# GpSimd pauses after every fourth gather of a group in the edge passes of a graph network

## The chip, the cores and the metric

One core of a Trainium2 chip runs the whole program. Its engines are TensorE (PE), VectorE (DVE), ScalarE (ACT), GpSimd (POOL) and SyncE (SP), each with its own instruction stream; 16 DMA engines serve them all. The metric is the device time of one execution in microseconds.

## The reference, cut to what matters

The reference chains four graph layers over 6250 nodes of 128 features and 100000 edges, sorted by destination. The change lies in the code of the first two.

```
# first network: 4 layers of attention over the edges
scores = sum(Q[dst] * K[src], -1) * scale
e = exp(scores - segment_max(scores)[dst]);  attn = e / segment_sum(e)[dst]
messages = segment_sum(attn * V[src], dst)
h = layernorm(h + messages @ WO + bO)
# second network: 8 heads of 16 features, 2 relations
score = sum(q[dst] * k_r[src], -1) ...;  alpha = e / den[dst]
out += segment_sum(v_r[src] * alpha, dst)
```

For each edge, then, a row of a node table is fetched by the number of its source node, multiplied with a row of its destination, turned into a weight, and the weighted rows are added up by destination. The third and fourth networks are sums over edges as well, in another function.

## The kernel before, in words

The edges of the first two networks are laid out in a list of *groups*. A group has S = 16 columns of 128 edges, one edge to each of the 128 partitions. `edge_pass` (L1797) walks the list two groups at a time (q = 0 and q = 1), each with its own buffers `meta[q]` (four words for each edge, among them the row number) and `rows[q]` (the fetched rows). It is called four times with mode "attend", once for each layer of the first network, and once with mode "heads" for the second. In the profiled execution an attend pass has 19 pairs of groups (18 with sorting work and dense work beside them, one without) and the heads pass 25.

What each engine does for a group:

- SP loads `meta[q]`, two words and the reset marks (L1951 to L1954), once DVE and PE have both counted `read[q]` for the group that last used the buffers.
- POOL waits until that load has landed (`listed[q]`), waits for `weighted`, which says that the buffer `rows[q]` is free again, and then issues 16 gathers, one for each column (L1973). A gather is an indirect DMA that brings 128 rows from the table in HBM: 512 bytes each in attend, 1024 bytes in heads. Each pair of columns counts on one semaphore, `got[q][j // 2]`, by 16 for each gather, so 32 for each pair. In heads the free buffer is awaited in two halves (L1971, at j = 0 and j = 8). In the 18 sorting pairs, and in group q = 1 alone, POOL after the gather of j = 3 waits for `evicted` and issues one scatter (L1979).
- DVE waits for `got[q][j // 2]` at every even column, multiplies each column with its query row (`prod`, L2369, or L2372 in heads), and between the columns does steps of the sort and of a dense part (masks L2250, sums L2260). `evicted` is given in step 5 of the sort, which comes after column 11 of group q = 0. After column 15 it makes the exponents (L2382 to L2401) and gives `scored`, and then adds the sums of the group before (L2213, L2214). In heads it also multiplies the fetched rows with the weights (`once_weighted`, L2429), which gives `weighted`.
- ACT takes the exponential (L2132) and scales the 16 columns (`weighted_rows`, L2140 in attend, L2193 in heads). In attend this gives `weighted`: then POOL may fill that `rows[q]` again.
- PE adds each weighted column into its sums (`ps_total`, L2037), and in attend also does the scores, transposes and sums of the dense part (L2047 to L2073).

So `rows` is a double buffer: the gathers of a group run while the group before is multiplied and weighted. The order on each queue is fixed by the program; nothing moves at run time. The counter `passed` is only counted up after a wait and is awaited by nobody.

Outside these passes POOL also gathers (L1532, in the two passes over tiles at the end) and scatters (L2963, L3321 and others); those lines are not touched.

Of the kernel before, what the change touches and what calls it, by code (L numbers as in the profile page):

```python
# [92 lines left out]
def open_stage(nc, ctx, names):  # L93
    names = [*dict.fromkeys([*names, "passed"])]
    sems = {n: ctx.enter_context(nc.semaphore(fresh(nc, n))) for n in names}
    nums = [sem.num for sem in sems.values()]
    sems["all"] = range(min(nums), max(nums) + 1)
    return sems
# [1698 lines left out]
def edge_pass(nc, k, mode, table_d, table_rows, width, list_d, words_d, resets_d, sched, fetch=None, sort=None, room=None, dn=None):  # L1797
# [13 lines left out]
    with ExitStack() as s:  # L1811
        m = open_stage(nc, s, ["own", "listed0", "listed1", "read0", "read1", "scored", "powered", "weighted", "routed", "summed",
                               "block_summed", "sum_taken", "passed", "dve_passed", "pe_passed", "fetched", "sorted", "totals", "before",
                               "spread", "placed", "evicted", "scattered", "x_loaded0", "x_loaded1", "xt_ps", "xt", "asked", "asked_ps", "asked_t",
                               "mask0", "mask1", "dense_ps", "masked", "dense_power", "power_ps", "power_t", "dense_summed", "dense_taken"]
                       + [f"got{q}{b}" for q in range(2) for b in range(B)])
        listed, read = [m["listed0"], m["listed1"]], [m["read0"], m["read1"]]
        got = [[m[f"got{q}{b}"] for b in range(B)] for q in range(2)]
# [78 lines left out]
        with nc.Block() as block:  # L1897
            @block.vector
            def _(dve):
                if mode == "heads":  # L1900
                    for r in range(2):
                        dve.memset(relation[:, r:r + 1], float(1 - r))
                if mode == "attend":
                    for q in range(2):
                        dve.memset(rows[q][:, :, P:P + 1], 1.0)
                    dve.memset(k.x1[:, :, P:P + 1], 1.0)
                    dve.memset(least[:, 0:1], BIG)
                if sort is not None:
                    dve.tensor_scalar(tile_no, k.iota_t[:], 1.0, None, ALU.add)
                    dve.tensor_copy(slot_no, so.slot_no[:])  # L1910
                    dve.tensor_copy(keep, so.keep[:].rearrange("p t c -> p (t c)"))
                for q in range(2):
                    dve.memset(resets[q][:, 0:1], HALF)
                    dve.memset(resets[q][:, S + 1:S + 2], HALF)
                    dve.memset(neg[q][:, :, S + 1:S + 2], HALF)
                dve.memset(neg[0][:, :, 0:1], HALF)

        with nc.Fori(0, epochs) as e:
# [3 lines left out]
            def turns(engine, body):  # L1922

                if sort is not None:
                    with engine.Fori(0, DENSE) as d:
                        for part in range(2):
                            body(d * 2 + part, True, d, part)
                    with engine.Fori(TURNS, pairs) as i:
                        body(i, False, None, None)
                else:  # L1930
                    with engine.Fori(0, pairs) as i:
                        body(i, False, None, None)

            with nc.Block() as block:
# [26 lines left out]
                @block.gpsimd  # L1961
                def _(pool):
                    def body(i, sorting, d, part):
                        for q in range(2):
                            pool.wait_ge(listed[q], i * 48 + 48)
                            if mode == "attend":
                                pool.wait_ge(m["weighted"], (i * 2 + (q + 1)) * WG)
                                pool.sem_inc(m["passed"], 1)
                            for j in range(S):
                                if mode == "heads" and j % HS == 0:  # L1970
                                    pool.wait_ge(m["weighted"], (i * 2 + q) * WG + (j // HS + 1))  # L1971
                                    pool.sem_inc(m["passed"], 1)
                                pool.indirect_dma_start(rows[q][:, j, 0:width], None, table_d,  # L1973
                                                        bass.IndirectOffsetOnAxis(meta[q][:, j, number:number + 1], 0)
                                                        ).then_inc(got[q][j // 2], 16)
                                if sorting and (q, j) == (1, 3):
                                    pool.wait_ge(m["evicted"], i + 1)
                                    pool.sem_inc(m["passed"], 1)
                                    pool.indirect_dma_start(so.list_d, bass.IndirectOffsetOnAxis(so.idx[:], 0), so.stretch[:], None  # L1979
                                                            ).then_inc(m["scattered"], 16)  # L1980
                    if sort is not None:
                        pool.dma_start(so.list_d[0:P], so.lane[:]).then_inc(m["scattered"], 16)
                    turns(pool, body)
                    if sort is not None:
                        pool.wait_ge(m["scattered"], 16 * TURNS + 16)
# [1664 lines left out]
```

## Time and profile before

| | us |
|---|---|
| median of three runs | 7428.16 (7428.05 to 7430.85) |
| span of the profiled execution | 10258.0 |

The profiled execution's own time is its span; it took 38% longer than the timed ones. How much of that lies where is part of the prediction's argument. Engine busy shares in it: PE 53%, DVE 43%, ACT 26%, POOL 45%. Times in the trace count from the start of the span. The four attend passes lie between 790 and 6450 us with a stage between layers after each, the heads pass between 6820 and 8390 us, and the two tile passes behind it. In a row of the trace, the number in square brackets is how long the engine sat idle before it, and behind the arrow stands what ended the idle time; "issue" means nothing that the profile shows.

### The profile page before, as it was taken

To read this page: it belongs to the slowest core of one execution; us is meant where nothing else is said; L and a number is where in the kernel's file an instruction comes from. 1 tells how busy PE (TensorE), PEld (TensorE's weight loads), DVE (VectorE), ACT (ScalarE), POOL (GpSimd) and SP (SyncE) were. 2 spreads that over 40 slices of the span, in tenths; PEclk is the share of its full clock that TensorE was granted. 3 is DMA by queue.
4 is the path that set the end of the run, shared out by engine and by line. 5 is a ranking of instruction groups with operands and counts; after the bars stand their busy time and mean duration, and the time that the engine had idled before them with its cause. 6 is when DMAs were issued, how large, how long until landed. Compare 5 with 4: busy or idle time off the path is not lost. (4 is left out here: it accounts for less than half of the span.)

```text
span 10258.0 us, 129339 instructions
## 1 busy us (share of the span) xinstructions
PE 5437.6 (53%) x28962; PEld 4358.8 (42%) x28963; DVE 4372.6 (43%) x13513; ACT 2633.3 (26%) x7476; POOL 4650.8 (45%) x4878
## 2 busy tenths in 40 slices
PE   4404555554555555455645454444444455886888
PEld 3203444443444444444534343322222234776777
DVE  7503444424444334444334443344444454444444
ACT  0102222232222222222322222213333333333111
POOL 1473444434444444444444445244445444444554
PEclk8556777767777667777667777666666666887888
DMA  4202222112222122222122222122222213222222
GB/s 155 69 0 60 57 56 59 54 47 56 57 55 56 42 61 55 57 58 56 33 68 57 55 57 54 32 85 67 68 68 70 69 49 91 61 62 56 65 66 58
DMA packets 404676, 615.62 MB, mean 60 GB/s; under 512 B 213466, under 2 KB 255993, under 8 KB 403884
## 3 DMA queue, kind: packets, MB, share of 16 engines
q0 software_dynamic: 169952, 363.29, 13.1%
q1 hardware_dynamic: 211126, 200.20, 7.0%
q10 hardware_dynamic: 23130, 47.29, 1.4%
q14 instruction: 345, 2.83, 0.1%
q8 instruction: 123, 2.02, 0.1%
HBM read 528.32 MB, written 82.09 MB: 60 GB/s over the span
## 5 line engine op out<-in xcount | busy, mean ns | idle before, releaser
L1973 POOL DMA_INDIRECT rows<-table_d,meta x2432 | 2308.2, 949 | 1648.2 <-ACT weighted_rows L2140 835.2
L2037 PE MATMUL ps_total<-weighted_rows,ident 128*128 128x129 f32 (+1 forms) x6464 | 1700.6, 417 | 2122.2 <-issue 1604.1
L2037 PEld LDWEIGHTS ps_total<-weighted_rows,ident 128*128 128x128 f32 x6464 | 1329.3, 270 | 2529.7 <-issue 2423.2
L2369 DVE SCALAR_TENSOR_TENSOR prod<-rows,q_rows 128x129 f32<-128x129 f32 x2432 | 695.4, 294 | 1510.9 <-issue 1346.1
L1973 POOL DMA_INDIRECT rows<-pairs_d,meta x800 | 769.9, 962 | 781.3 <-DVE once_weighted L2429 526.6
L2073 PE MATMUL dense_sums<-x_rows,dense_power_t 128*128 128x129 f32 x3528 | 593.5, 317 | 662.8 <-issue 293.2
L2158 ACT COPY dense_power_t<-dense_turned 128x512 f32<-128x512 f32 x504 | 264.8, 525 | 2371.5 <-PE dense_turned L2064 1658.7
L2073 PEld LDWEIGHTS dense_sums<-x_rows,dense_power_t 128*128 128x128 f32 x3528 | 528.6, 227 | 703.6 <-issue 580.6
L2140 ACT ACTIVATE weighted_rows<-rows,power 128x129 f32<-128x129 f32 x2432 | 733.3, 389 | 18.4 <-PE ps_total L2037 14.6
L1532 POOL DMA_INDIRECT tile_rows<-table_d,tile_halves x441 | 416.2, 944 | 427.3 <-PE tile_sums L1783 294.2
L2193 ACT ACTIVATE weighted_rows<-once_weighted,of_relation 128x136 f32<-128x136 f32 x1600 | 488.0, 393 | 454.6 <-DVE once_weighted L2429 422.7
L1532 POOL DMA_INDIRECT tile_rows<-made_d,tile_halves x441 | 416.7, 945 | 378.0 <-PE tile_sums L1783 245.6
L1979 POOL DMA_INDIRECT list_out_d<-sort_stretch,sort_idx x72 | 74.8, 1039 | 1111.7 <-DVEq L2321 1111.7
L2250 DVE CUSTOM_DVE_ANT_0 dense_masked<-dense_scores,dense_masked,dense_least 128x896 f32<-128x896 f32 x252 | 289.7, 1150 | 499.6 <-issue 229.0
L1773 PE MATMUL tile_sums<-near_rows,sums 128*128 128x129 f32 x2352 | 366.3, 293 | 170.1 <-issue 166.7
L2064 PE MATMUL dense_turned<-ident,dense_masked 128*128 128x128 f32 x1764 | 318.3, 301 | 217.4 <-issue 138.2
L2372 DVE TENSOR_TENSOR src_store<-rows,q_rows 128x128 f32<-128x128 f32 x800 | 209.9, 291 | 516.3 <-issue 499.3
L2053 PE MATMUL dense_scores<-sums,dense_asked_t 128*128 128x512 f32 x512 | 317.2, 704 | 161.0 <-DVE dense_least L2250 61.7
L1773 PEld LDWEIGHTS tile_sums<-near_rows,sums 128*128 128x128 f32 x2352 | 314.1, 202 | 202.7 <-issue 201.4
L1783 PE MATMUL tile_sums<-tile_rows,sums 128*128 128x129 f32 x1764 | 339.2, 357 | 103.9 <-issue 103.1
L2064 PEld LDWEIGHTS dense_turned<-ident,dense_masked 128*128 128x128 f32 x1764 | 225.3, 153 | 340.4 <-issue 199.2
L1783 PEld LDWEIGHTS tile_sums<-tile_rows,sums 128*128 128x128 f32 x1764 | 314.6, 267 | 128.5 <-issue 128.4
(700 smaller groups left out, 9515.6 us busy)
## 6 DMA issues: line engine op xcount, KB each, us to landing
dense_masked<-dense_masks_d SPq DMA_DIRECT2D x252, 448.0 KB
rows<-table_d,meta POOLq DMA_INDIRECT x2432
dense_masks_d<-unmasked ACTq DMA_DIRECT2D x9, 3136.0 KB
src_store<-near_window_d SPq DMA_DIRECT2D x50, 384.0 KB
near_window<-near_window_d SPq DMA_DIRECT2D x48, 384.0 KB
rows<-pairs_d,meta POOLq DMA_INDIRECT x800
tile_rows<-table_d,tile_halves POOLq DMA_INDIRECT x441
tile_rows<-made_d,tile_halves POOLq DMA_INDIRECT x441
```

The costliest lines, as they stand in the source:

```text
L1532: pool.indirect_dma_start(rows[b][:, c, 0:P], None, table_d, bass.IndirectOffsetOnAxis(meta[:, t, c:c + 1], 0)).then_inc(got[b] if t < T - ...
L1773: pe.matmul(total[:, q, 0:P + 1], spare[:, q, c, :], near_rows[q][:, c, :], start=(c == 0), stop=False)
L1783: mm = pe.matmul(total[:, q, 0:P + 1], spare[:, q, NEAR + c, :], rows[t % RB][:, c, :], start=False, stop=(c == FARC - 1))
L1973: pool.indirect_dma_start(rows[q][:, j, 0:width], None, table_d, bass.IndirectOffsetOnAxis(meta[q][:, j, number:number + 1], 0)).then_inc( ...
L2037: mm = pe.matmul(total[:, q, ds(part, 1), 0:W].rearrange("p a w -> p (a w)"), k.ident[:], wide[:, j % WS, :], start=False, stop=True, skip ...
L2053: pe.matmul(dense_ps[:, 0, :].rearrange("p (t c) -> p t c", c=P), asked_t[:], xt[:, t0:t0 + 4, :], start=True, stop=True)
L2064: mm = pe.transpose(power_ps[:, j * P:(j + 1) * P], masked[u % 2][:, c * P:(c + 1) * P], k.ident[:])
L2073: mm = pe.matmul(sum_ps[:, 0:P + 1], power_t[h][:, j, :], k.x1[:, u * UNIT + 4 * h + j, :], start=(h == 0 and j == 0), stop=(h == 1 and j ...
L2140: ins = act.activation(wide[:, j, :], rows[q][:, j, :], ACT.Copy, scale=power[q][:, 0, j + 1:j + 2])
L2193: ins = act.activation(wide[:, j % WS, r * HW:(r + 1) * HW], once[:, j].rearrange("p h d -> p (h d)"), ACT.Copy, scale=of_relation[q][:, j ...
L2250: dve.tensor_tensor_reduce(masked[u % 2][:], dense_ps[:].rearrange("p b c -> p (b c)")[:, 0:UW], masked[u % 2][:], 1.0, least[:, u:u + 1], ...
L2369: own(dve.scalar_tensor_tensor(prod[:, j % 2, :], rows[q][:, j, :], -1.0, query, ALU.mult, ALU.mult, accum_out=score[:, j, :]))
```

## The change

In both modes, before the gathers of columns 4, 8 and 12 of a group, POOL waits until the two pairs of columns issued last have landed, that is until `got[q][b]` has the value that DVE waits for too. Then it counts `passed` and goes on. Nothing is awaited after column 15. No other engine's code is touched.

```diff
                             for j in range(S):
                                 if mode == "heads" and j % HS == 0:
                                     pool.wait_ge(m["weighted"], (i * 2 + q) * WG + (j // HS + 1))
                                     pool.sem_inc(m["passed"], 1)
+                                if j % 4 == 0 and j:
+                                    for b in (j // 2 - 2, j // 2 - 1):
+                                        pool.wait_ge(got[q][b], i * 32 + 32)
+                                    pool.sem_inc(m["passed"], 1)
                                 pool.indirect_dma_start(rows[q][:, j, 0:width], None, table_d,
                                                         bass.IndirectOffsetOnAxis(meta[q][:, j, number:number + 1], 0)
                                                         ).then_inc(got[q][j // 2], 16)
```

## Rows read from the trace of the kernel before

**Rows 1.** Groups of POOL by line: busy and mean ns, then idle before
```profile
L1973 POOL DMA_INDIRECT rows<-table_d,meta x2432 | 2308.2, 949 | 1648.2 <-ACT weighted_rows L2140 835.2 <-issue 732.4 <-DMA resets<-resets_in_d 80.3
L1973 POOL DMA_INDIRECT rows<-pairs_d,meta x800 | 769.9, 962 | 781.3 <-DVE once_weighted L2429 526.6 <-issue 232.6 <-DMA resets<-resets_in_d 22.1
...
L1979 POOL DMA_INDIRECT list_out_d<-sort_stretch,sort_idx x72 | 74.8, 1039 | 1111.7 <-DVEq L2321 1111.7
```
**Rows 2.** The tile `rows`: ns min/median/max, first and last start in us
```profile
L1973 POOL DMA_INDIRECT rows<-table_d,meta x2432: 938/944/1336, 812.1 to 6413.4; - x188
L2369 DVE SCALAR_TENSOR_TENSOR prod<-rows,q_rows x2432: 264/294/371, 851.7 to 6437.3; 128x129 f32<-128x129 f32 x188
...
L1973 POOL DMA_INDIRECT rows<-pairs_d,meta x800: 940/946/1322, 6822.2 to 8358.2; - x160
```
**Rows 3.** POOL in order of time: the last gather of one layer, first of the next
```profile
2081.37 0.94 POOL L1973 DMA_INDIRECT rows<-table_d,meta  x1 [0.31 <-issue]
...
2251.38 0.98 POOL L1973 DMA_INDIRECT rows<-table_d,meta  x1 [12.87 <-DMA resets<-resets_in_d]
```
**Rows 4.** The longest waits: engine, line <- by what: us in total, times, longest
```profile
PEld ps_total L2037 <- issue: 2423.2, 993, 46.1
...
PE ps_total L2037 <- issue: 1604.1, 773, 4.8
DVE prod L2369 <- issue: 1346.1, 571, 25.7
```
**Rows 5.** DVE in order of time, around one group of an attend pass
```profile
4012.91 0.30 DVE L2369 SCALAR_TENSOR_TENSOR prod<-rows,q_rows 128x129 f32<-128x129 f32 x1 [4.61 <-issue]
...
4031.00 0.30 DVE L2369 SCALAR_TENSOR_TENSOR prod<-rows,q_rows 128x129 f32<-128x129 f32 x1 [1.86 <-issue]
...
4039.74 0.30 DVE L2369 SCALAR_TENSOR_TENSOR prod<-rows,q_rows 128x129 f32<-128x129 f32 x1 [3.03 <-issue]
```
**Rows 6.** Order of time: DVE and POOL in the first group of heads
```profile
6823.52 0.96 POOL L1973 DMA_INDIRECT rows<-pairs_d,meta  x1 [0.30 <-issue]
...
6826.04 0.95 POOL L1973 DMA_INDIRECT rows<-pairs_d,meta  x1 [0.30 <-issue]
6826.71 0.59 DVE L2372 TENSOR_TENSOR src_store<-rows,q_rows 128x128 f32<-128x128 f32 x2 [2.85 <-DMA rows<-pairs_d,meta]
...
6829.12 0.58 DVE L2372 TENSOR_TENSOR src_store<-rows,q_rows 128x128 f32<-128x128 f32 x2 [1.82 <-DMA rows<-pairs_d,meta]
```
**Rows 7.** DMA issues: engine, xcount, KB each, median us from issue to landing
```profile
tile_packed<-list_out_d SPq DMA_DIRECT2D x28, 31.5 KB, 2.2
```
**Rows 8.** Order of time: ACT frees a buffer, POOL starts the next group
```profile
2033.05 0.94 POOL L1973 DMA_INDIRECT rows<-table_d,meta  x1 [0.30 <-issue]
2037.04 4.80 ACT L2140 ACTIVATE weighted_rows<-rows,power 128x129 f32<-128x129 f32 x16
2042.62 0.99 POOL L1973 DMA_INDIRECT rows<-table_d,meta  x1 [8.63 <-ACT weighted_rows L2140]
2043.91 0.94 POOL L1973 DMA_INDIRECT rows<-table_d,meta  x1 [0.30 <-issue]
```
**Rows 9.** Order of time: POOL before, at and after one scatter
```profile
2003.73 0.94 POOL L1973 DMA_INDIRECT rows<-table_d,meta  x1 [0.30 <-issue]
2017.87 0.97 POOL L1979 DMA_INDIRECT list_out_d<-sort_stretch,sort_idx  x1 [13.19 <-DVEq L2321]
2019.15 0.97 POOL L1973 DMA_INDIRECT rows<-table_d,meta  x1 [0.30 <-issue]
```
**Rows 10.** The heads pass as one stretch: us, busy of PE, PEld, DVE, ACT, POOL
```profile
6820.00:8390.00 1570.00, 681.70 (x1734) 406.73 (x1735) 721.29 (x1675) 538.65 (x1670) 769.94 (x800) 0.61 0.24 68
```

## The prediction

> **What bounds the kernel now.** I read the groups by line for POOL first, since the change touches POOL alone. Its gathers of the edge passes number 2432 in attend and 800 in heads [rows 1]. A gather occupies POOL for 0.949 us, and the 732.4 us of "issue" idle over 2432 of them add 0.30 us, so one follows the other every 1.25 us; heads comes to (769.9 + 232.6) / 800 = 1.25 us as well. POOL's own work in the passes is then 2308.2 + 732.4 + 769.9 + 232.6 = 4043 us, and 74.8 + 72 x 0.30 = 96 us for the 72 scatters: 4140 us. Beside it the same rows show POOL waiting for others: 835.2 for ACT, 526.6 for DVE, 80.3 + 22.1 for the list, 1111.7 before the scatters, 2576 us together. By these rows alone POOL has slack everywhere, and a few microseconds more in a group would cost nothing.
>
> But the profiled execution is not the timed one. It has 10258.0 us, the median of the runs 7428.16, a difference of 2830 us. The reader should look for where an execution can lose that much. The list of waits shows it: PE before the edge sums and DVE before its products sit idle for "issue", nothing that the profile shows, 1604.1 and 1346.1 us, with 2423.2 us at PE's weight loads (these run beside PE's own) [rows 4]. In order of time these stalls come in stretches. One group takes DVE 4031.00 - 4012.91 = 18.1 us from first product to first product, with sort and dense steps in it, and in the next a single product waits 3.03 us for nothing [rows 5]. POOL keeps its 0.30 us all the while. I take the stalls for a load that profiling puts on the engines with many small instructions, and the timed runs as free of it.
>
> Then the passes can be timed. The attend gathers run from 812.1 to 6414.4 us [rows 2], less three stages between layers, each some 2251.38 - 2082.3 = 169 us as in the one shown [rows 3]: 5602 - 507 = 5095 us. Heads runs from 6822.2 to 8359.2 us, 1537 us. If everything outside takes equally long with and without profiling, the passes take 5095 + 1537 - 2830 = 3802 us in a timed run. That is 338 us less than POOL's own 4140. So POOL is all but saturated there, and its gathers even follow a little closer than in the trace: 3802 us without any waiting would be (3802 - 96) / 3232 = 1.147 us each. The 2576 us of waiting are, to 10%, the profile's own 2830 us. DVE is close behind: its group of 18.1 us stands against POOL's 16 x 1.147 = 18.4 us in attend. In heads the other engines are busy 681.70 (PE), 721.29 (DVE) and 538.65 us (ACT) for 50 groups, at most 14.4 us each, against 18.4 [rows 10].
>
> **The change, part by part.** *How many stops.* 2432 / 16 = 152 groups in attend and 50 in heads, three stops each: 606. In the 72 groups with a scatter the stop before column 4 stands behind the scatter; that leaves 534 full stops.
>
> *What a full stop costs.* POOL's queue runs dry, so three terms follow the fourth gather. First its landing. In the first group of heads DVE waits for the rows themselves: the gather of column 1 ends on POOL at 6823.52 + 0.96 = 6824.48 and DVE starts at 6826.71, 2.23 us later; the gather of column 3 ends at 6826.99 and DVE starts at 6829.12, 2.13 us later [rows 6]. This holds DVE's own start as well, so the landing is at most 2.2 us behind the gather's end. From below, a plain load of 31.5 KB takes 2.2 us from issue to landing [rows 7]; if a gather (64 KB in attend, 128 KB in heads) took that from its start, it would land 2.2 - 0.95 = 1.3 us after its end. I take 1.5 us in attend and 1.7 in heads, between the two, with less for the shorter rows. Second the restart: ACT has done its columns at 2037.04 + 4.80 = 2041.84 and the released gather starts at 2042.62, 0.78 us later [rows 8]. Third, the 0.30 us between gathers is no longer paid: so 1.5 + 0.78 - 0.30 = 2.0 us in attend and 2.2 in heads. The bounds are 1.3 + 0.78 - 0.30 = 1.8 and 2.2 + 0.78 - 0.30 = 2.7 us. The two waits and the count are three short instructions that end with the last of them; I put them at nothing beside these.
>
> The Trainium skill (DMA: Bandwidth & Descriptors, Anatomy of one DMA, SWDGE path) puts the fixed cost of a GpSimd DMA at about 2.0 us, most of it the receipt of the last write, plus bytes over 436 GB/s. Counted from the gather's start that would be 2.15 us for 64 KB; the trace has 0.96 + 2.23 = 3.2 us including DVE's start [rows 6], so the rule fits only if it is counted from the gather's end. By it a stop would be 2.15 + 0.78 - 0.30 = 2.6 us and 534 stops some 1400 us.
>
> *The stop behind the scatter.* The gather of column 3 is followed by 0.30 + 0.97 us of scatter [rows 9], so its landing (1.5) and the restart (0.78) reach 1.0 us past the scatter's end, less 0.30: 0.7 us where the scatter did not wait, and 0.9 with a landing of 1.7. In the trace it waits 13.19 us in the instance shown, and the stop would be free. I take 0.85, 72 x 0.85 = 61 us.
>
> *Who waits behind POOL.* Queued behind the stop are the rest of the group's gathers, the scatter, and the next group. DVE's products of columns 4 to 15 come later, then the exponents, ACT's weighting and PE's sums: all of the group's work hangs on it, and with a double buffer the group after next too. What could cover a stop is POOL's idle time in a timed run alone.
>
> *The sum.* 152 x 3 - 72 = 384 stops x 2.0 = 768; 150 x 2.2 = 330; with 61 it is 1159 us on POOL. The cover depends on how dense the gathers are in a timed run. At 1.147 us it is nothing. At the other bound, 0.95 us with no gap, POOL needs 3232 x 0.95 + 75 = 3145 us of 3802 and idles 657, but a stop then saves no 0.30 us. I take 1.10 us, nearer to the rows' 1.25: POOL needs 3232 x 1.10 + 86 = 3641 us and idles 161, all of which I count as cover, and each stop costs 0.15 us more, 80 us. So 1159 + 80 - 161 = 1078 us. With 7428 that is 8506; I say 8500 us, 14.4% more. The profiled execution won't show this sum against its own 10258 us: there the 2576 us of waiting are cover, and most of the 1159 us should go into them.
>
> **The rivals.** *DVE sets the pace and hides much.* In the low case, gathers at 0.95 us, 657 us of cover and stops at 1.8 + 0.30 = 2.1 us, the cost is 534 x 2.1 - 657 = 464 us: about 7900 us. For it speaks DVE's 18.1 us in a group [rows 5]; against it that POOL's spacing never moves from 1.25 us in the trace, even where nothing else presses. Up to about 8050 I count to this case.
>
> *All is hidden.* If the timed runs had the trace's slack, 1159 us would go into 2576 and nothing would change: 7428 us. Against it stands the time itself: a timed run lacks these 2576 us.
>
> *Faster: shorter gathers.* A gather may be slowed by those still in flight before it. With at most four in flight the 0.30 us between them could go. The place is all 3232 gathers, the price at most 3232 x 0.30 = 970 us, which gives 7428 + 1159 - 970 = 7617; it decides only where the spacing inside a four falls from 1.25 to below 1.25 - 1159 / 3232 = 0.89 us, and then by little: at 0.87 some 7360 us. Against it: the gathers right after a pause of 8.63 us follow at 2043.91 - 2042.62 = 1.29 us, no closer than in the middle of a run [rows 8]. A kin of it is the SBUF interface. The products have a median of 294 ns and a minimum of 264 [rows 2], so a quieter POOL gives DVE at most 2432 x 0.03 = 73 us, off the bound besides.
>
> **How the numbers follow.** Saturated POOL, 8050 us and above: 84 in 100. DVE's pace, 7445 to 8050: 11. All hidden: 3. Faster: 2. What this measurement can tell from no change is about 0.2%, 15 us. So slower has 0.95, within 0.2% 0.03, faster 0.02. Upwards the range has the dear stop: 534 x 2.7 with 72 x 1.5 is 1550 us and 8980 with no cover, which takes both bounds at once; 8750 stands for about 2.5 us a stop. Downwards it goes to 8030, a stop of 1.8 us with half of the 657 us as cover (534 x 2.1 - 330 = 790 us, 8220) and something more.
>
> **What would show it.** In the changed kernel's trace POOL's gathers come in fours at 1.25 us, with some 2.3 us (2.0 + 0.30) of idle before columns 4, 8 and 12 that DMA landings end; a group without other waits takes 20 + 6 = 26 us. POOL's waits for ACT, DVE and the scatter's release shrink from 2576 us by the better part of 1159, and the profiled span grows by well under 1078 us. The step on the landing is wrong if that idle is under 1.8 or over 3.0 us. The argument as a whole is wrong if the timed difference is under 450 us: then POOL had slack in the timed runs and the 2830 us lie elsewhere. If it is over 1400, a delayed group costs more than its own delay, through the double buffer.

## The result and the profile after

The changed kernel takes 8355.45 us (median of 4 runs, 8327.22 to 8365.57) against 7429.51 us before (median of 4, 7428.05 to 7432.45): 926 us more, ratio 1.125, 95% interval 1.1233 to 1.1266. I forecast 8500.

The profiled execution of before, with 10258.0 us, ran under other conditions than the timed runs: on one of the three chips used below this kernel takes about 10283 us in its timed runs as well, on the two others about 7406 us. So I compare the trace of after (span 8346.2 us) with a trace of before from a chip like the timed runs' own, called *before, clean* below (it is the run before_third): span 7409.7 us, timed runs there 7404.82 us.

The page of after, groups of POOL by line (busy, mean ns, then the idle time before them and what ended it), beside [rows 1]:
```profile
L1977 POOL DMA_INDIRECT rows<-table_d,meta x2432 | 2324.1, 956 | 1714.3 <-DMA rows<-table_d,meta 886.2 <-issue 753.9 <-DMA resets<-resets_in_d 51.6
L1977 POOL DMA_INDIRECT rows<-pairs_d,meta x800 | 781.1, 976 | 607.9 <-DMA rows<-pairs_d,meta 388.9 <-issue 204.6 <-DMA resets<-resets_in_d 14.3
...
L1983 POOL DMA_INDIRECT list_out_d<-sort_stretch,sort_idx x72 | 70.7, 982 | 29.2 <-DMA rows<-table_d,meta 21.9 <-issue 4.6 <-DVEq L2325 2.7
```
The same groups in before, clean:
```profile
L1973 POOL DMA_INDIRECT rows<-table_d,meta x2432 | 2309.2, 950 | 1102.7 <-issue 708.3 <-ACT weighted_rows L2140 328.8 <-DMA resets<-resets_in_d 63.2
L1973 POOL DMA_INDIRECT rows<-pairs_d,meta x800 | 777.9, 972 | 257.8 <-issue 242.9 <-DMA resets<-resets_in_d 14.3 <-DVE once_weighted L2429 0.6
...
L1979 POOL DMA_INDIRECT list_out_d<-sort_stretch,sort_idx x72 | 71.4, 991 | 64.5 <-DVEq L2321 43.6 <-issue 20.9
```
These lines give most of the account. In attend POOL's idle time before gathers and scatters goes from 1102.7 + 64.5 to 1714.3 + 29.2 us, 576 more, and its busy time grows by 14. In heads it goes from 257.8 to 607.9, 350 more, and 3 busy. The waits on landings are new, 886.2 and 388.9 us; the wait for ACT, 328.8 us, has all but left (22.6 us, 13 times, in the rows of the tile). And before, clean has not 2576 us of waiting for others but 328.8 + 63.2 + 14.9 + 43.6 = 451 (14.9 is 14.3 for the list and 0.6 for DVE in heads, 43.6 the wait before the scatters).

The tile `rows` (ns least/median/most, start of the first and the last in us), beside [rows 2], in after:
```profile
L1977 POOL DMA_INDIRECT rows<-table_d,meta x2432: 942/947/1331, 799.8 to 5314.8; - x188
...
L1977 POOL DMA_INDIRECT rows<-pairs_d,meta x800: 943/949/1653, 5657.7 to 7031.4; - x160
```
and in before, clean:
```profile
L1973 POOL DMA_INDIRECT rows<-table_d,meta x2432: 938/944/1296, 800.4 to 4733.3; - x188
...
L1973 POOL DMA_INDIRECT rows<-pairs_d,meta x800: 942/946/1517, 5076.0 to 6096.3; - x160
```
Attend grows from 3933.8 to 4516.0 us, and without the three turns between layers (440.1 and 429.2 us in the traces) from 3494 to 4087. Heads grows from 1021 to 1375 us. That is 593 + 353 = 946 us in the passes, while the two spans differ by 936.5. A second trace of after, taken on the same chip as before, clean (the run after_again), has 580 + 352 = 932 us in the passes and a span that is 943.9 us longer. So what moved outside the passes is some 10 us, once one way and once the other.

POOL in order of time in after (start, duration, idle before it and what ended it), a scatter and the gathers around it, beside [rows 8, 9]:
```profile
2488.66 0.94 POOL L1977 DMA_INDIRECT rows<-table_d,meta  x1 [0.30 <-issue]
2489.90 0.98 POOL L1983 DMA_INDIRECT list_out_d<-sort_stretch,sort_idx  x1 [0.30 <-DMA rows<-table_d,meta]
2491.87 0.98 POOL L1977 DMA_INDIRECT rows<-table_d,meta  x1 [0.98 <-issue]
...
2495.65 0.94 POOL L1977 DMA_INDIRECT rows<-table_d,meta  x1 [0.30 <-issue]
2498.95 0.94 POOL L1977 DMA_INDIRECT rows<-table_d,meta  x1 [2.36 <-DMA rows<-table_d,meta]
2500.20 0.94 POOL L1977 DMA_INDIRECT rows<-table_d,meta  x1 [0.30 <-issue]
```
A full stop shows as 2.36 us of idle in place of 0.30: 2.06 us. That is the median in attend; in heads it is 2.56, so 2.26. Behind the scatter the stop leaves 0.98 us here. From the end of the gather of column 3 to the start of that of column 4 it is 2491.87 - 2489.60 = 2.27 us here, 2.36 in the median and 1.59 in before, clean, 0.77 us more. Inside a four the spacing stays at 1.25 us.

The tile passes behind heads, as one stretch (length, busy PE, PEld, DVE, ACT, POOL, granted clock, DMA share, GB/s), in after and then in the first profile of before:
```profile
7050.00:8346.00 1296.00, 1139.15 (x9556) 1095.73 (x9554) 831.29 (x1451) 460.05 (x1382) 887.53 (x935) 0.92 0.34 92
```
```profile
8390.00:10258.00 1868.00, 1393.97 (x9545) 1288.11 (x9543) 852.51 (x1451) 461.77 (x1369) 884.36 (x935) 0.82 0.24 64
```
The change touches nothing here, yet the first profile has 572 us more for nearly the same instructions (the stretches are cut at slightly different points). This pair says that the two executions ran under different conditions.

### The profile page after: what moved, and what is told of

The parts are those of the page before. It is cut to its first block and busy times, and to the rows that moved or that the text cites. A ratio compares the mean times of both kernels' runs of the same rounds, so it can differ in the third digit from the quotient of the medians.

```text
span 8346.2 us, 130046 instructions
## 1 busy us (share of the span) xinstructions
PE 4890.3 (59%) x28962; PEld 4062.1 (49%) x28963; DVE 4330.2 (52%) x13513; ACT 2630.1 (32%) x7476; POOL 4679.0 (56%) x4878
## 5 line engine op out<-in xcount | busy, mean ns | idle before, releaser
L1977 POOL DMA_INDIRECT rows<-table_d,meta x2432 | 2324.1, 956 | 1714.3 <-DMA rows<-table_d,meta 886.2
L2041 PE MATMUL ps_total<-weighted_rows,ident 128*128 128x129 f32 (+1 forms) x6464 | 1426.7, 386 | 1307.0 <-ACT weighted_rows L2197 843.9
L2041 PEld LDWEIGHTS ps_total<-weighted_rows,ident 128*128 128x128 f32 x6464 | 1211.5, 248 | 1527.9 <-issue 1387.6
L1977 POOL DMA_INDIRECT rows<-pairs_d,meta x800 | 781.1, 976 | 607.9 <-DMA rows<-pairs_d,meta 388.9
L2077 PE MATMUL dense_sums<-x_rows,dense_power_t 128*128 128x129 f32 x3528 | 645.7, 337 | 789.3 <-DVE dense_rows L2264 654.2
L2077 PEld LDWEIGHTS dense_sums<-x_rows,dense_power_t 128*128 128x128 f32 x3528 | 576.8, 245 | 829.8 <-issue 811.1
L2150 ACT ACTIVATE dense_shrink<-dense_least 128x1 f32<-128x1 f32 x252 | 74.0, 293 | 829.3 <-DVE dense_least L2254 829.2
L1758 PE MATMUL near_gathered<-q_rows,near_hot 128*128 128x128 f32 x2352 | 275.7, 278 | 73.8 <-DVE near_hot L1622 73.8
L1758 PEld LDWEIGHTS near_gathered<-q_rows,near_hot 128*128 128x128 f32 x2352 | 271.4, 195 | 74.3 <-DVE near_hot L1622 67.8
L1758 PE MATMUL near_gathered<-x_rows,near_hot 128*128 128x128 f32 x2352 | 276.5, 278 | 32.4 <-DVE near_hot L1622 32.4
L1758 PEld LDWEIGHTS near_gathered<-x_rows,near_hot 128*128 128x128 f32 x2352 | 270.9, 195 | 37.7 <-DVE near_hot L1622 25.5
```

The source lines that it names most:

```text
L1758: mm = pe.matmul(gathered[:, h, at:at + P], near_hot[i][:, c % 2, j, :], table[:, WIDE * c + j, 0:P], start=(j == 0), stop=(j == WIDE - 1) ...
L2041: mm = pe.matmul(total[:, q, ds(part, 1), 0:W].rearrange("p a w -> p (a w)"), k.ident[:], wide[:, j % WS, :], start=False, stop=True, skip ...
L2077: mm = pe.matmul(sum_ps[:, 0:P + 1], power_t[h][:, j, :], k.x1[:, u * UNIT + 4 * h + j, :], start=(h == 0 and j == 0), stop=(h == 1 and j ...
```

## The experiments

Three groups of runs, each against before on the same chip. I call the chip of the first group A, the others B and C.

**Chip A: before 10283.02 us (10271.78 to 10318.67).**

*before_again*, the kernel before, unchanged.

> The kernel before, unchanged, for a second profile of it. The first one took 10258 us, that of the changed kernel only 8346 us, as long as its timed runs, and its waits of POOL for others are gone. Theory 1 (POOL's queue sets the pace, with some waiting left that the stops could use): if this profile comes out near the timed 7429 us, POOL's gathers still follow at 1.25 us and its waits in the passes sum to some 300 to 500 us, since the passes without any waiting would take 4140 us and 2893 us lie outside them in the changed kernel: 7429 - 2893 - 4140 = 396. Theory 2 (another engine sets the pace): waits of POOL well over 500 us and a spacing below 1.25 us. If it comes out near 10258 again, it tells only that profiling itself is what stretches this kernel.

It took 10255.85 us with a span of 10254.4. An execution with the profiler and the timed ones agree to 0.3%. The 2830 us between my profile and my times are thus no cost of profiling. They go with the chip: all seven timed runs of before are slow on A, and none on B and C. But each of the three chips was used in one session only, so whether the chip itself is slow or was in a passing condition is not shown.

*heads_only*, stops in the heads pass alone. (What I expected of this run and the next two holds for a chip on which before takes 7429 us, so their numbers can't be held against these results.)
```diff
-if j % 4 == 0 and j:
+if mode == "heads" and j % 4 == 0 and j:
```


> The three stops in the heads pass alone. The changed kernel's heads pass takes 1375 us (27.5 us a group), the sum of 16 x 1.25, three stops of some 2.5 us idle and a little. Theory 1: before, POOL alone set the pace there too, 20.1 us a group, 1003 us in all; the price is some 340 to 370 us, 7770 to 7800. Theory 2: before, the chain over DVE and ACT set 22 to 23 us a group, and 100 to 150 us of the stops are covered: +220 to +270, 7650 to 7700.

It took 10103.54 us, ratio 0.9811 (0.9785 to 0.9837): 180 us *faster* than before on this chip. The tile `rows` in heads, in before_again and then in heads_only:
```profile
L1973 POOL DMA_INDIRECT rows<-pairs_d,meta x800: 942/948/1330, 6819.9 to 8354.6; - x160
```
```profile
L1977 POOL DMA_INDIRECT rows<-pairs_d,meta x800: 940/946/1699, 6838.0 to 8210.8; - x160
```
The pass goes from 1536 to 1374 us, and 1374 is what it takes with stops on the other chips too. Without stops it takes 1021 there and 1536 here. So the stops take away all that chip A adds to heads.

*attend_only*, stops in attend alone.
```diff
-if j % 4 == 0 and j:
+if mode == "attend" and j % 4 == 0 and j:
```


> The stops in the four attend passes alone. Theory 1: POOL saturated before, 783 us a pass of its own work against 1022 in the changed kernel: + up to 956, but the two kernels together have to give 926, so with heads at 350 it should be about +575, 8005. Theory 2 (heads cheap): +660 to +700. In both the sum with the heads-only kernel is 926 within 30 us, since the passes are separated by barriers; a sum over 1000 or under 850 would show that something outside the passes changed.

It took 9436.60 us, ratio 0.9172 (0.9148 to 0.9196): 846 us faster. The waits that nothing in the profile explains (us, times, longest) shrink from before_again:
```profile
PE ps_total L2037 <- issue: 1625.2, 759, 5.1
DVE prod L2369 <- issue: 1377.6, 555, 25.8
```
to attend_only:
```profile
DVE prod L2373 <- issue: 640.5, 329, 7.3
PE ps_total L2041 <- issue: 607.4, 336, 6.1
```
In before, clean the wait of DVE's products for "issue" is 350.3 us.

*one_stop*, one stop in a group, before column 8, in both passes.
```diff
-if j % 4 == 0 and j:
+if j == 8:
```


> One stop in each group, before column 8, in both modes: 202 stops instead of 606. A stop costs POOL 2.06 us in attend and 2.26 in heads (idle of 2.36 and 2.56 less the 0.30 between gathers), 426 us. Theory 1, cover of about 396 us spread evenly, 2 us a group: the first stop is nearly free, +30 to +150, 7460 to 7580. Theory 2, no cover and each stop cheap: a third of 926, +309, 7738. Theory 3, the cover sits only in a few groups: +300 to +426.

It took 9918.14 us, ratio 0.9632 (0.9607 to 0.9656), 365 us faster. On chip A a third of the stops gives 365 of the 1026 us (180 + 846) that the two halves above give together. None of this bears on the timed result, in which before takes 7429.51 us. It says what the first profile showed, and that the price of a stop has to be read elsewhere.

**Chip B: before 7404.82 us (7399.35 to 7424.62).**

*before_third*, before unchanged: the trace called before, clean.

> The kernel before, for a profile on this chip. If the kernel before times at 7429 here, the trace should have no register instruction of 0.70 us, POOL's spacing at 1.25 us and its waits in the passes at 300 to 500 us: theory 1, the cover that the first experiments could not see. If it times at 10283, the trace repeats the first.

7411.18 us with a span of 7409.7. Why its passes have slack is seen in POOL's order of time, the last gather of one group and the first of the next:
```profile
2333.90 0.94 POOL L1973 DMA_INDIRECT rows<-table_d,meta  x1 [0.31 <-issue]
2345.90 0.94 POOL L1973 DMA_INDIRECT rows<-table_d,meta  x1 [11.06 <-ACT weighted_rows L2140]
```
Groups start 20.2 us apart in the median (16 x 1.25 and a little, POOL saturated) until one waits up to 11.1 us for ACT. In the list of waits this is:
```profile
POOL rows L1973 <- ACT weighted_rows L2140: 328.8, 66, 11.1
```
Of these 66 only 36 are waits: they last 8.9 us in the mean, 320 us together, and the other 30 are the usual 0.30 us. In order of time the 36 stand at one fixed place, the first group of every second sorting pair, so one group in four waits.

*after_again*, the changed kernel unchanged.

> The changed kernel, unchanged, timed again beside the kernel before on one chip. On the chip of the first four experiments the kernel before took 10283 us in each of seven runs, not 7429, and its trace there has the same long idle of DVE and PE for nothing shown as the first profile (single register and semaphore instructions of 0.70 instead of 0.04 us, from some 6 us after the start of an unbroken run of gathers to 1 or 2 us after its end). Theory A: the stalls belong to the chip, not to profiling. Then on such a chip the changed kernel is the faster one: attend alone gave -846 us and heads alone -180, together -1026, 9250 us against 10283; on a chip without the stalls it is 8355 against 7429 as first measured. Theory B: the stalls were a passing condition of the job, the kernels give 7429 and 8355 on every chip.

8365.76 us, ratio 1.1299 (1.128 to 1.1318): 961 us, with a span of 8353.6. The result holds on a second chip.

*by_twos*, a stop before every second column, seven in a group.
```diff
-if j % 4 == 0 and j:
-    for b in (j // 2 - 2, j // 2 - 1):
-        pool.wait_ge(got[q][b], i * 32 + 32)
+if j % 2 == 0 and j:
+    pool.wait_ge(got[q][j // 2 - 1], i * 32 + 32)
```


> A stop after every second gather, seven in each group instead of three: 1414 stops. Each costs POOL 2.06 us in attend and 2.26 in heads. On a chip without the stalls: POOL is saturated after three stops, so four more in each of 152 and 50 groups cost 152 x 4 x 2.06 + 50 x 4 x 2.26 = 1705 us over the 8355, 10060 us; if POOL still had cover, less. On a chip with the stalls: if they need an unbroken run of more than two gathers none is left, and the time is the same 10060 us within 1%, while the kernel before takes 10283.

10177.33 us, ratio 1.374 (1.3717 to 1.3763). Against after_again that is 1811.6 us for 202 x 4 = 808 further stops, 2.24 us each (I had expected 1705). This is the price of a stop by dose, with at most the 23 us of waiting for ACT that after_again still has as cover. By pass it is 1395 us for 608 stops in attend, 2.29 each, and 448 for 200 in heads, 2.24. POOL in attend:
```profile
L1976 POOL DMA_INDIRECT rows<-table_d,meta x2432 | 2321.2, 954 | 3107.8 <-DMA rows<-table_d,meta 2571.0 <-issue 483.7 <-DMA resets<-resets_in_d 53.2
```
No wait for ACT is among its releasers any more.

*first_pair*, the same three places, but waiting only for the older two of the last four gathers.
```diff
-for b in (j // 2 - 2, j // 2 - 1):
+for b in (j // 2 - 2,):
```


> As the change, but each stop waits for the older two of the last four gathers alone. By POOL's end of the fourth gather these have been landed for about 1 us (they end 2.5 us before it and land 1.5 behind their end), so POOL has at most a short pause, from the restart of 0.78 us: 0 to 0.8 us a stop. Without the stalls: +0 to +100 us over 7429, since up to 2 us a group are covered: 7430 to 7530. With the stalls: theory P (a pause in POOL's stream is what ends them): little change, 10000 to 10283; theory Q (the number of gathers handed ahead to POOL's queue is what brings them): as good as the full stops or better, under 9300.

7442.93 us, ratio 1.0049 (1.0032 to 1.0065): 38 us. The instructions of the change are nearly all there, and two gathers are still queued or landing when POOL waits. So the 961 us are the emptied queue (landing and restart), not the extra waits and counts: these cost 38 / 606 = 0.06 us each in time. POOL's idle time before its gathers grows by 33 us in attend and 9 in heads, while its wait for ACT falls by 24, so without cover it would be some 65 us, 0.11 each.
```profile
L1977 POOL DMA_INDIRECT rows<-table_d,meta x2432 | 2312.1, 951 | 1135.2 <-issue 706.9 <-ACT weighted_rows L2144 304.6 <-DMA rows<-table_d,meta 64.1
```
The wait for ACT is back at 304.6 us.

**Chip C: before 7407.86 us (7397.80 to 7418.08).**

*attend_only_b*, the edit of attend_only.

> The stops in attend alone, on a chip without the stalls: from the traces of both kernels the attend passes take 3494 us before and 4074 after, the heads pass 1021 and 1373. So +580 us here and +350 left for heads, if the passes don't touch each other; theory 2 (something of the price lies outside the passes) would give a sum with heads that differs from +950 by over 30. On a chip with the stalls 0.917 repeats.

8010.65 us, ratio 1.0803 (1.0783 to 1.0822): 603 us, attend 4090 us long, heads 1021. Where the full change costs 926 to 961, that leaves some 320 to 360 us for heads.

*one_stop_b*, the edit of one_stop.

> One stop in each group, before column 8, as before, hoped for on a chip without the stalls, where the kernel before takes 7405 to 7430 us. Its 50 stops in heads are not covered, 50 x 2.26 = 113 us. In attend 152 stops cost POOL 2.08 us each, 316 us. Theory 1 (the 329 us that POOL waits for ACT there are cover until they are used up): the attend stops nearly vanish, +115 to +190 us in all. Theory 2 (a stop delays the group's own chain to ACT as well, so that POOL's wait for ACT hardly shrinks with the first stops): two thirds or more of it show, +320 to +430. If the chip is one with the stalls, the first measurement (0.963) repeats.

7706.21 us, ratio 1.0389 (1.0366 to 1.0412): 298 us, which lies between my two theories and fits neither. Against before, clean the passes grow by 165 us (attend, 152 stops) and 125 us (heads, 50 stops). In heads a stop costs 2.5 us, whole, and more than the 2.26 of the changed kernel: the idle before column 8, sixteen gathers after the last stop, has a median of 2.97 us, where three stops in a group gave 2.56. In attend a stop costs 1.08 us, about half.
```profile
L1977 POOL DMA_INDIRECT rows<-table_d,meta x2432 | 2314.0, 951 | 1271.1 <-issue 704.3 <-DMA rows<-table_d,meta 340.3 <-ACT weighted_rows L2144 167.7
```
The wait for ACT has gone from 328.8 to 167.7, and it is still the same 36 waits, now 4.66 us each in place of 8.9. From one of them to the next lie four groups with four stops, 4 x 2.06 = 8.2 us, and the wait shrinks by 4.2: about two stops of four are covered, the other two also delay the weighting that POOL waits for. That they do so through DVE's products is argued from the order of the program and not shown; the counts are in the traces.

*early_weigh*, the kernel before without stops, but ACT weights columns 8 to 15 of the pair's first group right behind 0 to 7, one step earlier. This takes away what POOL waits for.
```diff
-if u in (2, 3, UNITS - 1):
-    weigh_columns(i, 0, range(S // 2, S) if u == 3 else range(S // 2))
+if u in (2, UNITS - 1):
+    weigh_columns(i, 0, range(S) if u == 2 else range(S // 2))
```


> The kernel before, with one move on ACT: in the first pair of two, ACT weights columns 8 to 15 of group q = 0 right behind columns 0 to 7, and not after the next unit of dense powers. This frees rows[0] some 8 us earlier in every second pair, and POOL's wait for ACT (329 us in the passes, 8 to 11 us every second pair) should go to under 100; the dense chain is 2.5 us later. Theory 1 (POOL's queue and that wait set the pace of attend): -150 to -300 us, 7130 to 7280. Theory 2 (the dense chain over PE, DVE and ACT sets it, and POOL's wait for ACT is only its shadow): no gain or a small loss, -20 to +90.

7211.92 us, ratio 0.973 (0.9711 to 0.9749): 196 us faster than before, and the fastest kernel of this study.
```profile
L1973 POOL DMA_INDIRECT rows<-table_d,meta x2432 | 2309.0, 949 | 894.9 <-issue 725.4 <-ACT weighted_rows L2140 84.2 <-DMA resets<-resets_in_d 79.8
```
The wait for ACT is down by 245 us, and attend is 3290 us long instead of 3494, 204 less: POOL's queue, with this wait in it, sets the length of the pass. Of the 245 us 37 are back as other idle time before the gathers.

*early_weigh_stops*, that kernel with the stops of the change.

> The changed kernel with the same move on ACT. In it POOL hardly waits for ACT (23 us), so the move gives nothing: 8340 to 8380 us by both theories; against the early-weighing kernel the stops would then cost the full 1160 to 1240 us by theory 1, and about 930 to 960 by theory 2.

8339.18 us, ratio 1.1258 (1.124 to 1.1277): 1127 us over early_weigh, where the stops cost 926 to 961 over before. I had put 1160 to 1240 or 930 to 960; it is short of the first, but far nearer to it. And it ends only 16 to 27 us below the changed kernel's own times. So the slack that ACT left POOL was worth some 170 to 200 us of cover to the change, and the stops use it up whichever way ACT works.

## Why the prediction came out as it did

**Right: the price of a stop.** I took 2.0 us in attend and 2.2 in heads from a landing of 1.5 and 1.7, a restart of 0.78 and the 0.30 not paid. The trace of after has medians of 2.06 and 2.26, and by_twos has 2.24 over both. The terms hold one by one too: at the stops whose landing the trace can place, the fourth gather lands 1.60 us (attend) and 1.80 us (heads) behind its end on POOL, and the next one starts 0.76 us after that in both. The means are a little higher. Added up place by place along POOL's order of time, from before, clean to after, the idle at full stops goes from 117.0 to 959.1 us in attend, 842 for 384 stops, 2.19 each; behind the scatters from 21.9 to 74.6, 53 for 72; in heads from 45.7 to 388.9, 343 for 150, 2.29 each. Some waits are longer than the median, up to 5.2 us. The term 768 + 330 + 61 = 1159 us measured 842 + 343 + 53 = 1238, 7% more.

The two sides that the Trainium skill's rule gave (DMA: Bandwidth & Descriptors, Anatomy of one DMA, SWDGE path) bracket the measurement. The page of after has medians from issue to landing of 2.5 us in attend and 2.8 in heads:
```profile
rows<-table_d,meta POOLq DMA_INDIRECT x2432, 2.5
...
rows<-pairs_d,meta POOLq DMA_INDIRECT x800, 2.8
```
By the rule the estimate is 2.15 us for 64 KB and about 2.3 for 128 KB if it is counted from the gather's start; counted from its end it gave a stop of 2.6 us, where 2.06 were measured. I had held that it fits only from the end; it fits from neither.

**Right: the stop behind the scatter**, 0.85 predicted, 0.77 measured; and its count, 606 stops with 72 such. *Right: the waits and counts are nearly free*, by first_pair. *Right: the slack that only the trace had is no cover in a timed run.*

**Wrong: "I take the stalls for a load that profiling puts on the engines ... and the timed runs as free of it."** The second half held, the first fell with before_again: the timed runs on chip A are as slow as its profile. One trace and one list of times from elsewhere can't tell the two apart; the tile passes, untouched by the change and 1868 against 1294 us long, do as soon as both sides have a trace.

**Wrong, therefore: "everything outside takes equally long with and without profiling", passes of 3802 us.** Outside takes 7410 - 3494 - 1021 = 2895 us, and my split gave 7428 - 3802 = 3626. Of the 2830 us, some 730 lay there and not in the passes. The passes take 4515 us.

**Wrong, therefore: gathers 1.10 us apart in a timed run.** They are 1.25 apart, as in every trace. I derived the closer spacing from the 3802 us, against the rows that never showed it. The term of 80 us measured nothing.

**Wrong: the cover of 161 us.** Along POOL's order of time the idle at the starts of attend's groups went from 353.8 us to 69.4, that before the scatters from 64.5 to 29.2, and that at the starts of the layers from 54.0 to 51.6: 322 us of cover. In heads there is none: waits of 14.9 before and 14.3 after. I had both passes saturated alike; heads is, attend has one late buffer in every second pair.

The balance: 1238, and 11 us inside the fours, less 322 is 927 us of idle time, beside which POOL is busy 17 us longer; the timed runs have 926 to 961. Mine was 1159 + 80 - 161 = 1078. The 151 us between are 90 too little on the price (79 at the stops, 11 inside the fours), 80 too much on the spacing and 161 too little cover. The measured time lies nearer to the forecast than the reasoning deserved: the same wrong 3802 us gave a spacing too short and a cover too small, and no row stood behind the cover.

**Wrong: the signs in the profile that used the slack.** "The profiled span grows by well under 1078 us" can't be tested as put: the first profile and that of after are from different conditions, and the span fell from 10258.0 to 8346.2 us. Profile to profile on B and the chip of the timed runs the span grows by 936.5, as the timed runs do. That the waits for ACT, DVE and the scatter's release shrink is right, but from 451 us and not from 2576. The idle before columns 4, 8 and 12, "some 2.3 us", and "20 + 6 = 26 us" for a group are right: 2.36, and 26.3 to 26.5 in attend.

**The rivals.** *DVE's pace hides much* holds in a small form: the engine is ACT, its price some 320 us of cover and not 657. *All is hidden* is out for this time. It has the right form on chip A, where the halves are even faster than before; whether the whole change is faster there was not run. *Shorter gathers* is out: the spacing inside a four is 1.25 us. DVE's products have a median of 294 ns as before.

## What to carry to other kernels

A stop in which GpSimd waits for its own gathers costs their landing and its restart, here 2.1 to 2.3 us (2.5 in heads with sixteen gathers before it), whole wherever GpSimd sets the pace; a wait that leaves two gathers in flight cost 0.06 us. When a profile's span and the timed runs differ, compare a stage that the change doesn't touch before any term is derived from the difference, and keep durations that every row shows (1.25 us) over one that such a derivation asks for. Slack on the pacing engine is worth removing for itself: moving ACT's weighting one step forward gave 196 us.

## What the runs showed of the hardware

Chip A ran the same program 39% slower than B and C (10283 against 7405 and 7408 us). In its records register, move and semaphore instructions of DVE, PE and SyncE's sequencers that take 0.02 to 0.07 us elsewhere take about 0.70 us in part of the passes: counted between 0.55 and 0.76 us, they sum to 1522 us on DVE, 681 on PE and 235 on SyncE, in before_again, and to 1 us each on DVE and PE in before, clean. In the median the first comes 6.4 us after the start of a run of gathers without a pause, and the last ends 2.3 us after its last gather. The stops take them away in heads (404 us on DVE in before_again, 1 in heads_only) and thin them out in attend (1116 us on DVE, 296 in attend_only), and both kernels are faster there. How long a run has to be is not shown: with nothing awaited after column 15, runs of eight gathers stay in both passes, and in heads they leave none. These records come together with a lower granted clock in a stage without edge gathers (0.81 against 0.92) that such records don't explain: the tile passes take 1864 us on A and 1294 on B, and on A they hold 12 us of them. What is different on that chip, or was in that session, was not tried and stays open.
